# A two-layer recurrence on one core: the second gate sum split in two, and the input and connecting products spread over the halves of the steps

## The reference, cut to what matters

```python
def _run_layer(x_seq, Wx, Wh, b):
    gx = jnp.einsum('btd,dg->btg', x_seq, Wx) + b
    gx = jnp.swapaxes(gx, 0, 1)
    def step(carry, gx_t):
        h, c, m = carry
        g = gx_t + h @ Wh
        i = jax.nn.sigmoid(g[:, 0 * h_dim:1 * h_dim])
        f = jax.nn.sigmoid(g[:, 1 * h_dim:2 * h_dim])
        c_tilde = jnp.tanh(g[:, 2 * h_dim:3 * h_dim])
        o = jax.nn.sigmoid(g[:, 3 * h_dim:4 * h_dim])
        m_new = jnp.tanh(g[:, 4 * h_dim:5 * h_dim])
        c_new = f * c + i * c_tilde
        h_new = o * jnp.tanh(c_new) + m_new
        return ((h_new, c_new, m_new), h_new)
    ...
h1 = _run_layer(x, Wx0, Wh0, b0)
h2 = _run_layer(h1, Wx1, Wh1, b1)
return jnp.einsum('bth,ho->bto', h2, Wfc) + bfc
```

## Time and profile before

| what | us |
|---|---|
| median of 3 runs | 1110.24 (1110.03 to 1111.13) |
| profiled execution, its time | 1110.15 |
| its span | 1108.2 |
| busy in the span: PE | 896.5 (81%) |
| PE weight loads | 721.4 (65%) |
| DVE | 784.1 (71%) |
| ACT | 556.8 (50%) |
| POOL | 331.9 (30%) |

### The profile page before, as it was taken

How to read it: one execution, slowest core, us unless ns; L and a number is a source line. 1 busy time by engine, 2 the same in 40 slices (tenths; PEclk the granted TensorE clock), 3 DMA queues, 4 the chain that set the end, 5 groups by cost and what they waited for, 6 DMA issues and landing times.

```text
span 1108.2 us, 43614 instructions
## 1 busy us (share of the span) xinstructions
PE 896.5 (81%) x17230; PEld 721.4 (65%) x17230; DVE 784.1 (71%) x2835; ACT 556.8 (50%) x1629; POOL 331.9 (30%) x481
## 2 busy tenths in 40 slices
PE   3667768267787788773599999999999999989997
PEld 1346545135555555551489999999999988847786
DVE  3458984986655555556678888887788888755877
ACT  0446667125455444532354455555544455545886
POOL 0326656555565565540001111111111111020321
PEclk9769997569999998995699999999999999998999
DMA  8700005201222221216000000000000000002232
GB/s 237 271 1 2 1 30 171 62 25 38 65 66 63 65 65 44 59 34 160 19 4 0 0 0 0 0 0 0 0 0 0 0 0 0 1 2 87 94 140 75
DMA packets 26707, 52.07 MB, mean 47 GB/s; under 512 B 4528, under 2 KB 17816, under 8 KB 26648
## 3 DMA queue, kind: packets, MB, share of 16 engines
q1 hardware_dynamic: 21656, 41.04, 11.3%
q0 software_dynamic: 4992, 10.23, 3.5%
HBM read 44.02 MB, written 7.24 MB: 46 GB/s over the span
## 4 chain that ended last, share of the span: by engine, by line
PE 38%; DVE 10%; issue 7%; ACT 0%; DMA 0%; POOL 0%; DVEq 0%; ACTq 0%
PE quad L1330 19%; PE bank L1330 8%; DVE post L1480 3%; DVE post L1518 2%; PE quad L318 1%; PE bank L318 1%; PE quad L320 1%; PE quad L319 1%; DVE post L1524 1%; PE bank L319 1%; PE bank L320 1%; DVE post L1519 1%; PE quad L1340 1%; PE quad L1628 1%; PE bank L1360 0%
## 5 line engine op out<-in xcount | busy, mean ns | idle before, releaser
L1330 PE MATMUL quad<-post,area 128*128 128x32 f16 (+1 forms) x7520 | 230.2, 182 | 24.7 <-DVE post L1524 18.1
L1330 PEld LDWEIGHTS quad<-post,area 128*128 128x128 f16 x7520 | 213.1, 96 | 41.6 <-DVE post L1524 41.3
L1330 PE MATMUL bank<-post,area 128*128 128x32 f16 (+1 forms) x6260 | 193.2, 180 | 6.7 <-DVE post L1524 4.4
L1330 PEld LDWEIGHTS bank<-post,area 128*128 128x128 f16 x6260 | 176.9, 96 | 12.3 <-DVE post L1524 5.0
L1417 ACT ACTIVATE post<-post 128x96 f32<-128x96 f32 x252 | 71.3, 283 | 171.1 <-DVE post L1480 171.1
L1313 POOL COPY post<-post 128x32 f32 (+1 forms) x126 | 30.8, 245 | 381.8 <-DVE post L1524 381.8
L868 POOL DMA_INDIRECT y_scratch<-area x78 | 76.9, 985 | 88.7 <-DVE area L1209 78.6
L1508 DVE SCALAR_TENSOR_TENSOR post<-post 128x32 f32<-128x32 f32 x252 | 48.4, 192 | 75.6 <-ACT post L1427 75.6
L957 PE MATMUL quad<-w0s,area 128*128 x312 | 61.6, 277 | 49.2 <-DVE area L1209 49.2
L1480 DVE TENSOR_REDUCE post<-bank 128x96 f32<-128x192 f32 x252 | 80.7, 320 | 6.4 <-PE bank L1330 4.8
L1220 DVE SCALAR_TENSOR_TENSOR area<-bank,area 128x512 f32<-128x512 f32 x78 | 53.9, 691 | 43.8 <-ACT area L1033 21.3
(11 more groups left out here) (255 smaller groups left out, 1940.4 us busy)
## 6 DMA issues: line engine op xcount, KB each, us to landing
w0s<-in_w SPq DMA_DIRECT2D x12, 768.0 KB, 12.3
area<-mask_scratch SPq DMA_DIRECT2D x7, 1008.0 KB, 4.6
area<-in_rec SPq DMA_DIRECT2D x7, 640.0 KB
post<-y_scratch SPq DMA_DIRECT2D x16, 252.0 KB
area<-in_w SPq DMA_DIRECT2D x4, 768.0 KB
post<-in_f SPq DMA_DIRECT2D x8, 256.0 KB, 4.4
area<-in_patches SPq DMA_DIRECT2D x1, 1488.4 KB
area<-in_taps SPq DMA_DIRECT2D x1, 1350.0 KB
```

The lines of the kernel that those rows point to most:

```text
L1330: mm = pe.matmul(at[0][:, at[1] + out.start:at[1] + out.stop], rec_w[:, w, s, m * P:(m + 1) * P], operand, start=False, stop=False, skip_g ...
```

## The change

The y sum becomes two reductions of 64 elements a partition: the output gate's stays where it was, the memory's goes behind new_cell. sum_y now counts two for each step. On ScalarE the memory tanh moves behind tanh of the cell and signals the same semaphore tanh_c, which so counts two for each step as well; store_state waits for it besides its old wait. On TensorE the input products go as 12 matmuls (IFC) in even steps and 8 (OM) in odd ones, and the connecting products as 12 in even steps (IFC of k = 0), then, in odd steps, 10 behind the input products (OM of k = 0 and the first chunk of k = 1) and 18 behind layer 1's own products. The number of matmuls is the same as before.

```diff
-            IFC, OM = range(XCH), range(XCH, GCH)
+            IFC, OM, FIRST = range(XCH), range(XCH, GCH), range(1)
+
+            def from_first(q, k, which):
+
+                return chunks(1, 1 - q, WX1 + k, hpair0[:, 1 - q, k].rearrange("p s g b -> p (s g b)"), BOTH, which)
...
-                    pe.wait_ge(sg("sum_y0"), SEQ - 2 if j < 2 else SEQ)
+                    pe.wait_ge(sg("sum_y0"), 2 * (SEQ - 2 if j < 2 else SEQ))
...
-                    chunks(0, 1 - q, WX0, xcur[:, 1 - q], BOTH, range(odd * GCH // 2, (odd + 1) * GCH // 2))
+                    chunks(0, 1 - q, WX0, xcur[:, 1 - q], BOTH, OM if odd else IFC)
+                if odd and here(t, PAIR, SEQ + 1):
+                    from_first(q, 0, OM)
+                    from_first(q, 1, FIRST)
...
-                    for which, name in ((IFC, "pre_x1"), (OM, "pre_y1")):
-                        mm = chunks(1, 1 - q, WX1 + odd, hpair0[:, 1 - q, odd].rearrange("p s g b -> p (s g b)"),
-                                    BOTH, which)
-                        if isinstance(t, int) and t == PAIR + 1:
-                            mm.then_inc(sg(name), 1)
+                    if odd == 0:
+                        from_first(q, 0, IFC)
+                    else:
+                        for which, name in ((IFC[1:], "pre_x1"), (OM, "pre_y1")):
+                            mm = from_first(q, 1, which)
+                            if isinstance(t, int) and t == PAIR + 1:
+                                mm.then_inc(sg(name), 1)
...
-            def gates_y(l, n):
-                act.wait_ge(sg(f"sum_y{l}"), n)
+            def gate_out(l, n):
+                act.wait_ge(sg(f"sum_y{l}"), 2 * n - 1)
                 act.activation(gates[:, l, OUT:OUT + SW], pre[:, l, 3 * SW:4 * SW], ACT.Sigmoid, scale=UNSCALE)
-                act.activation(gates[:, l, MEM:MEM + SW], pre[:, l, 4 * SW:5 * SW], ACT.Tanh, scale=UNSCALE)
+
+            def memory(l, n):
+                act.wait_ge(sg(f"sum_y{l}"), 2 * n)
+                act.activation(gates[:, l, MEM:MEM + SW], pre[:, l, 4 * SW:5 * SW], ACT.Tanh, scale=UNSCALE
+                               ).then_inc(sg(f"tanh_c{l}"), 1)
...
                         gates_x(l, n)
-                        gates_y(l, n)
+                        gate_out(l, n)
                         cell_of(l, n)
+                        memory(l, n)
...
-            def sum_part(l, n, u, name):
+            def sum_part(l, n, u, name, first=0, count=XCH):
 
                 x, y = pair_banks(l, u // PAIR)
-                src, lo, count = (x, 0, XCH) if name == "x" else (y, XCH, GCH - XCH)
+                src, lo = (x, first) if name == "x" else (y, XCH + first)
...
-                                  src[:, 0:count * 64].rearrange("p (m s g b) -> p s m b g", m=count, s=PAIR, g=2
-                                                                 )[:, u % PAIR], AX, ALU.add
+                                  src[:, first * 64:(first + count) * 64].rearrange(
+                                      "p (m s g b) -> p s m b g", m=count, s=PAIR, g=2)[:, u % PAIR], AX, ALU.add
...
-                dve.wait_ge(sg(f"tanh_c{l}"), n)
+                dve.wait_ge(sg(f"tanh_c{l}"), 2 * n - 1)
...
                 dve.wait_ge(sg(f"part{l}"), n * 3 - 1)
+                dve.wait_ge(sg(f"tanh_c{l}"), 2 * n)
...
-                    sum_part(0, n0, u, "y")
+                    sum_part(0, n0, u, "y", 0, KH)
                 if ending:
                     store_low(1, n1 - 1, v)
                 if first_layer:
                     products(0, n0)
                     new_cell(0, n0)
+                    sum_part(0, n0, u, "y", KH, KH)
                     new_state(0, n0, u)
...
                 if second_layer:
-                    sum_part(1, n1, u, "y")
+                    sum_part(1, n1, u, "y", 0, KH)
                 if first_layer:
                     store_low(0, n0, u)
                 if second_layer:
                     products(1, n1)
                     new_cell(1, n1)
+                    sum_part(1, n1, u, "y", KH, KH)
```

## The result

The changed kernel takes 1096.64 us (median of 4 runs, 1094.48 to 1097.77) against 1110.39 (4 runs, 1110.03 to 1111.13): ratio 0.9869, 95% interval 0.9852 to 0.9886. It is faster by 13.75 us, where 17.8 were forecast. The time lies in the stated range.

The account below looks back on a forecast made before the run. Bound: the two-layer recurrence's loop through stores, y sum and own products, 1.719 us a half. Saving 0.074 us in each half of 120 steps gives 17.8 us: 1110.15 - 17.8 = 1092.4 us; stated range 1089 to 1107.5.

Parts of the forecast that it names:

- The loop: One layer's half step: x sum, other layer's stores and y sum, own products, x sum; 1.719 us, forecast to become 1.645.
- the second loop: Recurrence: x sum, cell products, new cell, new_state, x sum; 1.62 us before, forecast 1.56, below the loop that sets the half.
- the full slot of TensorE: Even step, layer 1: bias pair, 20 connecting products and weight loads fill 1.72 us without a gap.
- The short sum: 64-element y sum between full store and low store: 0.126 us instead of 0.20, gaining 0.074 a half, at most 0.08.
- rival B: No effect: a 64-element sum keeps VectorE 0.20 us, or new_state's 0.20 holds the half; 1110 us, chance 0.08.
- the bound of the low store: On VectorE: the low store starts no sooner than 0.22 us after the full store, whose output it reads.
- The memory half of the sum: Between new_cell and new_state on VectorE: costs nothing under 0.26 us of cover; 0.13 us a half without cover.
- ScalarE and the second wait: Memory tanh ends 0.67 us after new_cell, slack at least 0.2; the high store's second wait taken as 0, bounds 0 and 0.06.
- Rivals A and C: Store's second wait: A, 0.06 us a half, 1106.8 us, chance 0.12; C, VectorE's queue held, 1121.2 us, chance 0.10.
- TensorE's order: Products spread 12, 12, 18, 18 over the halves: slots of 1.47 and 1.58 us, both fitting under 1.645.
- Without this part the even step would hold the half at 1.72: Without the new spread of products on TensorE, the even step stays at 1.72 us and nothing is gained there.
- the forecast's own range: Whole time 1089 to 1097 us, the upper edge standing for a 64-element sum 0.02 us dearer; forecast's chance 0.70.

Follow-up runs that it names:

- e4: Kernel before, with the low weight term of chunk 0 left out of the own products (two matmuls fewer); ratio 0.9895, 3.338 us a step.
- e11: Changed kernel, with the low weight term of chunks 0 to 2 left out of the own products (six matmuls fewer); ratio 0.967, 3.136 us a step.
- e3: Kernel before, with only the new order of products on TensorE and no split of the y sum; ratio 0.9992, 3.436 us a step.
- e5: Changed kernel, with both short sums together ahead of the low store; ratio 1.0127 to the kernel before, 3.561 us a step.
- e6: Kernel before, with a second, already met wait added in store_state; ratio 1.0015, 3.437 us a step.
- e2: Changed kernel, with the old order of input and connecting products on TensorE (split only); ratio 0.9890 to the kernel before, 3.339 us a step.

## Why the prediction was right, point by point

**The loop.** It is confirmed as it was set up: 1.652 us a half against 1.645. e4 shows TensorE's part on it, e11 the second loop at 1.568 against the predicted 1.56, and e3 that the full slot of TensorE cost the kernel before no more than 0.006 us in one half of four.

**The short sum, the mis-sized term.** 0.126 us was read off a line through 192 and 128 elements. From the start of a short sum ahead of a low store to the start of that store it is 0.1345 us in the mean of the 240 halves, against 0.2009 for the sum of 128 elements before. The gain is 0.2009 - 0.1345 = 0.0664 us a half, times 240 = 15.9 us; measured are 15.98. That is 1.8 of the 4.1 us by which the forecast of 17.8 missed 13.75. The floor of 0.20 (rival B) did not come in, and the bound of the low store (0.22 behind the full store) wasn't reached: it is now 0.237.

**The memory half of the sum.** It costs nothing behind new_cell, and 0.13 us a half without its cover (e5), both as stated. The rule that was weighed against the change, minimize the number of operations (the Trainium skill, page "VectorE: DVE Perf Modes", section "Rules for kernel authors"), holds in e5, where the added one lies on the path, and not in the changed kernel, where VectorE has 252 more operations and the program is 14 us faster. The prediction gave that page's section "The DRAIN you can't avoid" of the Trainium skill without its exception, that a next operation which isn't held starts earlier; the distance of 0.10 us behind an operation of 0.18 fits the exception.

**ScalarE and the second wait.** The memory tanh ends at 705.42, 0.59 us after new_cell, before even the x sum (705.51) that stands ahead of the store. No idle time appears at the high store: it starts 0.275 us behind the x sum, as before. Rivals A and C had their price from a place where a wait blocked; e6 gives 0 where none does.

**TensorE's order.** Slots of 1.47 and 1.58 us were forecast. By their weight loads they are 1.54 us in the even step (704.71 to 706.25, gap 0.11) and 1.58 in the odd one (gap 0.075 in the mean). The even one is 0.07 longer than forecast, 0.06 of it because 0.031 us a product was read from start to start, while the 20 loads of the earlier trace rows run 0.06 us into the next ones (705.96 + 0.68 = 706.64 against 706.58). Both still fit, so it changed nothing. "Without this part the even step would hold the half at 1.72" is e2. But the prediction gave this part no price of its own: 4 us of the 16 hang on it.

**What the sum left out.** It took everything outside the two-layer steps as unchanged. The steps at the end gave 0.7 us (0.4 of them the clock's), the recurrence of this execution began 1.0 earlier, and the tail took 3.3 back, since the clock was at half for 17.1 us instead of 10.2. One profile of before could not show that this tail varies by 3 us between executions, and that it had caught the cheapest of the ten profiled here. The measured 1096.64 lies even in the forecast's own range, which ended at 1097. But that edge stood for a short sum 0.02 us dearer, and the sum was only 0.009 dearer; the rest of the miss came from work that the prediction took as unchanged. So the size of the recurrence's gain was right within a tenth, and that the whole time fell inside the narrow range is in part luck.

## What to carry to other kernels

Where each engine works in a fixed order, take the distances from start to start, and compare each with the same pair in a stretch where one partner is idle: here 0.20 against 0.11 us gave away a wait for TensorE that the view of waits did not list. An operation on the loop that isn't needed at once is worth splitting if, and only if, the second part finds a gap that stays covered; and before shortening a loop, look for the engine whose slot is as long as the loop, since that one decides how much of the gain arrives: here it cost 0.006 us in one half before and would have cost 0.07 after. Check stretches behind the change for the granted clock before giving them a cause.

## What the runs showed of the hardware that was not expected

Start to start behind a VectorE reduction out of PSUM: 0.275 us for 192 elements, 0.201 for 128, 0.135 for 64; the steps are 0.074 and 0.066, so it isn't quite a line. A second wait that is already met costs nothing measurable on a store next to a running 192-element sum (3.437 against 3.438 us a step). On new_state, whose other wait blocks, it goes with 0.06 us more (0.55 us behind new_cell instead of 0.49). The last stage, with the same instructions, takes 119.7 to 123.1 us by how long TensorE's clock is granted at half (10.2 to 17.1 us). With two products of no use in an idle time of 2.3 us the clock was at half for 6.8 us, and the stage took 118.45.
